# Attention matmuls issued two key chunks behind the scores instead of four, and a reciprocal in two halves, in a pre-norm transformer layer

## What is computed

```python
def attn(x, wq, bq, wk, bk, wv, bv, wo, bo):
    q = einsum('bsd,hde->bhse', x, wq) + bq      # k and v alike
    scores = softmax(einsum('bhse,bhte->bhst', q, k) * 0.125, axis=-1)
    att = einsum('bhst,bhte->bhse', scores, v)
    return att.transpose(0, 2, 1, 3).reshape(b, s, 1024) @ wo.T + bo

def ffn(x):
    h = silu(lin(x, w1)) * lin(x, w2)            # 1024 -> 4096
    h = gelu(lin(h, h1)); h = gelu(lin(h, h2))   # 4096 -> 4096
    return lin(h, w3)                            # 4096 -> 1024

x = x + attn(layernorm(x), ...)
x = x + ffn(layernorm(x))
```

## Time and profile before

| | us |
|---|---|
| median of the two runs shown | 4151.65 (4062.03 and 4241.27) |
| the profiled execution, device time | 3774.29 |
| its span, slowest core (core 7) | 3772.8 |
| spans of the 8 cores | 3759.9 to 3772.8 |
| mean granted TensorE clock of the cores | 0.949 to 0.951 |

### The profile page before, as it was taken

How to read it: one execution, slowest core, us unless ns; L and a number is a source line. 1 busy time by engine, 2 the same in 40 slices (tenths; PEclk the granted TensorE clock), 3 DMA queues, 4 the chain that set the end, 5 groups by cost and what they waited for, 6 DMA issues and landing times.

```text
span 3772.8 us, 35110 instructions; the slowest of 8 cores (3759.9 to 3772.8 us)
## 1 busy us (share of the span) xinstructions
PE 3342.6 (89%) x14676; PEld 1374.5 (36%) x14676; DVE 485.9 (13%) x491; ACT 824.3 (22%) x740; POOL 151.8 (4%) x291
## 2 busy tenths in 40 slices
PE   2377878787768599999999999999999999999999
PEld 0132222222213144444444444444444444444444
DVE  0542222222224413100000000000310000000000
ACT  1106666666761130000000000003000000000000
POOL 0000000000000011000000000001100000000000
PEclk9688989898988699999999999999999999999999
DMA  6000000000102355544444444455554444444445
GB/s 157 0 1 1 1 1 1 1 1 1 23 1 101 97 73 76 93 73 75 78 78 77 73 75 77 85 136 76 75 90 75 78 79 78 72 75 78 78 77 130
DMA packets 49613, 237.41 MB, mean 63 GB/s; under 512 B 7777, under 2 KB 7842, under 8 KB 28338
## 3 DMA queue, kind: packets, MB, share of 16 engines
q0 software_dynamic: 40208, 193.08, 30.1%
q1 hardware_dynamic: 9250, 42.08, 3.3%
HBM read 411.19 MB, written 16.78 MB: 113 GB/s over the span
## 4 chain that ended last, share of the span: by engine, by line
PE 65%; DVE 1%; DMA 1%; ACT 0%; issue 0%; DVEq 0%; ACTq 0%; POOLq 0%
PE ps_f L1167 64%; DMA wb<-h 1%; DVE act_bf L194 1%; PE ps_r L1091 0%; PE ps_m L1087 0%; ACT hbufA L1191 0%; DVE ostg L1218 0%; ACT hbufB L1191 0%; DVEq L193 0%; ACTq L1183 0%; DVEq L1217 0%; DVEq L1215 0%; DVEq L1205 0%; DVEq L1204 0%; POOLq L1132 0%
## 5 line engine op out<-in xcount | busy, mean ns | idle before, releaser
L1167 PE MATMUL ps_f<-hbufB,wb 128*128 128x512 bf16 x5120 | 1109.1, 380 | 11.4 <-DMA wb<-h 8.4
L1167 PE MATMUL ps_f<-hbufA,wb 128*128 128x512 bf16 x4096 | 884.4, 379 | 2.9 <-ACT hbufA L1191 2.9
L1167 PEld LDWEIGHTS ps_f<-hbufB,wb 128*128 128x128 bf16 x5120 | 501.5, 98 | 618.9 <-issue 17.9
L846 ACT ACTIVATE pbuf<-ps_sc,cneg 128x1024 bf16<-128x1024 f32 x512 | 551.8, 1112 | 262.4 <-PE ps_aO L456 250.6
L1167 PEld LDWEIGHTS ps_f<-hbufA,wb 128*128 128x128 bf16 x4096 | 400.6, 98 | 486.7 <-issue 3.9
L1167 PE MATMUL ps_f<-act_bf,wb 128*128 128x512 bf16 x2048 | 451.7, 383 | 19.4 <-DVE act_bf L194 14.3
L456 PE MATMUL ps_aE<-pbuf,vt_sb 128*65 128x512 bf16 x512 | 226.2, 442 | 87.7 <-DVE q_sb L830 87.6
L1167 PEld LDWEIGHTS ps_f<-act_bf,wb 128*128 128x128 bf16 x2048 | 200.8, 98 | 272.3 <-issue 36.2
L435 PE MATMUL ps_sc<-q_sb,k_sb 64*128 64x512 bf16 x1024 | 216.2, 413 | 88.0 <-ACT pbuf L846 78.7
L1218 DVE SCALAR_TENSOR_TENSOR ostg<-ps_f,s_sb,x2rb 128x1024 f32<-128x1024 f32 x16 | 20.6, 1285 | 1987.8 <-PE ps_f L1167 1987.8
L1191 ACT ACTIVATE hbufB<-ps_f,sh_sb 128x1024 bf16<-128x1024 f32 x64 | 71.3, 1114 | 816.0 <-PE ps_f L1167 816.0
(11 more groups left out here) (96 smaller groups left out, 934.4 us busy)
## 6 DMA issues: line engine op xcount, KB each, us to landing
wb<-h POOLq DMA_DIRECT2D x128, 1024.0 KB, 8.0
wb<-w POOLq DMA_DIRECT2D x128, 256.0 KB, 4.2
wb<-w POOLq DMA_DIRECT2D x16, 1024.0 KB, 9.0
xrb<-xst SPq DMA_DIRECT2D x8, 1024.0 KB, 4.8
x2hbm<-x2buf SPq DMA_DIRECT2D x8, 1024.0 KB, 14.5
x2rb<-x2hbm SPq DMA_DIRECT2D x16, 512.0 KB, 9.3
out_fm<-ostg SPq DMA_DIRECT2D x16, 512.0 KB, 8.5
wqld<-wq POOLq DMA_DIRECT2D x1, 2048.0 KB, 16.6
```

What stands on the lines that cost most here:

```text
L846: sc.activation(pbuf[:, (c % 4) * 1024:(c % 4) * 1024 + 1024], ps_sc[:, (c % 2) * 1024:(c % 2) * 1024 + 1024], AF.Exp, bias=cneg[:, j:j + ...
L1167: ins = t.matmul(ps_f[:, (i % 2) * 1024 + nn * 512:(i % 2) * 1024 + (nn + 1) * 512], wb[i % 3][:, k * 128:(k + 1) * 128], rhs[:, k * rstri ...
```

## The change

The order on PE within a unit is rewritten. All 16 scores of a unit are issued in its own loop. With c = 0 and 1 come the attention matmuls of chunks 14 and 15 of the unit before, and from c = 2 those of chunk c-2. The keys of `side` now stand for c itself, so each side item comes two chunks earlier. The last unit issues its last two attention matmuls behind the loop, as before. The waits inside the emit functions are as they were, and so are all buffers. (The branch for items of kind "v" is never taken: no `side` list holds one.)

The reciprocal and its bf16 copy are done for columns 0 to 1023 and then for 1024 to 2047, four vector instructions instead of two, and each ps_rep matmul waits for the half that it reads.

```diff
-                            if I == 0:
-                                emit_scores(t, 0, 0)
-                                emit_scores(t, 0, 1)
-                            for c in range(2, TC):
+                            for c in range(TC):
                                 emit_scores(t, I, c)
-                                if c == 2 and I >= 1:
-                                    emit_att(t, I - 1, TC - 2)
-                                elif c == 3 and I >= 1:
-                                    emit_att(t, I - 1, TC - 1)
-                                if c >= 4:
-                                    emit_att(t, I, c - 4)
-                                for item in side.get(c - 2, ()):
+                                if c <= 1 and I >= 1:
+                                    emit_att(t, I - 1, TC - 2 + c)
+                                if c >= 2:
+                                    emit_att(t, I, c - 2)
+                                for item in side.get(c, ()):
...
-                            if I < NI - 1:
-                                emit_scores(t, I + 1, 0)
-                                emit_att(t, I, TC - 4)
-                                emit_scores(t, I + 1, 1)
-                                emit_att(t, I, TC - 3)
-                            else:
-                                emit_att(t, I, TC - 4)
-                                emit_att(t, I, TC - 3)
+                            if I == NI - 1:
                                 emit_att(t, I, TC - 2, exp_wait=True)
                                 emit_att(t, I, TC - 1, exp_wait=True)
...
+                rhv = [0, 0]
...
-                    vop(v, "reciprocal", denom_sb, denom_sb)
-                    vop(v, "tensor_copy", rtile, denom_sb)
+                    for hf in range(2):
+                        vop(v, "reciprocal", denom_sb[:, hf * 1024:(hf + 1) * 1024],
+                            denom_sb[:, hf * 1024:(hf + 1) * 1024])
+                        rhv[hf] = vop(v, "tensor_copy",
+                                      rtile[:, hf * 1024:(hf + 1) * 1024],
+                                      denom_sb[:, hf * 1024:(hf + 1) * 1024])
...
-                    t.wait_ge(s_v, v0)
                     t.wait_ge(s_small, 16 * 11)
                     for j in range(NPAIR):
...
                         for nn in range(4):
+                            t.wait_ge(s_v, rhv[nn // 2])
                             ins = t.matmul(
```

More of the change, by code:

```diff
@@ L767, in _ @@
                                 side[1] = [("cr", jn)]
-                            if I == 0:
-                                emit_scores(t, 0, 0)
-                                emit_scores(t, 0, 1)
-                            for c in range(2, TC):
+                            for c in range(TC):
                                 emit_scores(t, I, c)
-                                if c == 2 and I >= 1:
-                                    emit_att(t, I - 1, TC - 2)
-                                elif c == 3 and I >= 1:
-                                    emit_att(t, I - 1, TC - 1)
-                                if c >= 4:
-                                    emit_att(t, I, c - 4)
-                                for item in side.get(c - 2, ()):
+                                if c <= 1 and I >= 1:
[3 more added lines that the diff above has]
+                                for item in side.get(c, ()):
                                     kind = item[0]
-                                    if kind == "proj":
+                                    if kind == "v":
+                                        emit_vchunk(t, item[1])
+                                    elif kind == "proj":
                                         emit_proj(t, item[1], item[2], item[3])
```

## The result

The changed kernel is faster: 3684.91 us in the median of 11 runs, against 4097.01 us for 10 runs of the kernel before. In 7 of the 10 runs before and 5 of the 11 after, the cores of one die or of both were granted a lower clock and took longer, whichever the kernel, so I compare the others: 3774 to 3775 us before, 3682 to 3685 us after. Their ratio is 0.9759, with a 95% interval of 0.9743 to 0.9776: 2.4% faster, 91 us of 3775. The profiled execution took 3685.35 us.

What follows compares the result with a forecast made beforehand. In the attention stage a chain of waits between PE and ACT sets the pace. Gains of 63 (steps), 1 (first unit) and 0.7 us (halves), 65 together, take 3774.3 to 3709 us; stated median 4080, range 3700 to 4200 us.

Steps and rivals of the forecast that it cites:

- the bound and the lag: Attention stage: with attention matmuls two chunks behind, ACT becomes the bound; a step falls from 1.15 to 1.007 us.
- the circle: Attention stage: loop of exp, score pair and attention pair, 2.30 us for two exps; without the attention pair 1.74 us.
- the drains' stall: Wait while DVE empties ps_aE and ps_aO between units: 2.64 us beyond a unit's 16 steps, against 2.73 before.
- the projection's own stall: Attention stage, 28 projections: each still holds up ACT about 3.04 us; moving earlier gains only the shorter steps, 0.55 us.
- PE sets that pace in both orders: Attention stage at PE's lower clock: chunks take 1.53 us either way, so 70 gain nothing, taking back 10 us.
- 3 us for the drains behind: Attention stage: 17 drains followed by the lower clock have a longer step after them, taking 3 us off the gain.
- Fewer: Rival, attention stage: no drain ends at the lower clock; gain about 100 us, 3674 us; chance 0.11.
- more drains end at the lower clock: Rival, attention stage: all 31 drains end low, 14 more losing 2.2 us each; gain 34 us, 3740 us; chance 0.18.
- the likeliest case: Whole kernel: the forecast gain of 50 to 85 us, 3689 to 3724 us; chance 0.60.

Runs made afterwards that it cites:

- a4: The kernel before with eight slots for the exponentials instead of four, order on PE unchanged; 3701.2 us.
- a1: The changed kernel with every side item two chunks later, where it was before; 3714.1 us.
- b4: The changed kernel with 10 additional score pairs in every drain of ps_aE and ps_aO, so that PE stays busy; 3647.8 us.
- a3: The kernel before with only the reciprocal and its copy in halves; 3773.8 us.
- b3: The changed kernel with the attention matmuls three chunks behind the scores instead of two; 3710.2 us.

## Why the prediction was right and wrong

**Right: the bound and the lag.** ACT waited for ps_aO because of the slot, the circle opened, PE's pace of 0.87 us fitted under ACT's, and the step fell from 1.15 to 1.00 us. a4 shows the cause by another way to the same step. The lag with the side items at their old place and the halves earns 60 us (a1); the forecast for lag and halves was 64.

**Right: the drains' stall hardly changes.** PE's wait for the casts is 87.2 us after, 87.6 before. The upper-clock step over a drain is 3.51 to 4.17 us in b4, 3.73 in the mean, where I worked out 3.65.

**Right: the halves, as far as can be seen.** Forecast 0.7 us, 0.45 in a3's timeline; in device time so little can't be told from nothing.

**Wrong: "Projections ... the projection's own stall stays about 3.04 us. So all 32 units gain the same."** It holds for 21 of 28. The first projection of each pair now starts with the table load, which the prediction's step never looked at: the load was in no row, and I put it into the forecast of idle time but not into the sum. Seven cases of 1.43 us are 10 us.

**Wrong: "PE sets that pace in both orders ... That takes back 70 x 0.143 = 10 us", and 3 us for the drains behind.** The pace at the lower clock is the same in both, as I said: 1.53 us. But I held the time at the lower clock at its old 166 us, and it fell from 158 to 115. At 0.35 us for each, as b4 gives it, 43 us are 15 us. The rival "Fewer" had the smaller time at the lower clock, with 0.11, and "more drains end at the lower clock" got 0.18, with the idle between S(2) and A(0) growing to 3.0 us as its ground; the clock went the other way. That idle grew only in three drains of the last pair, where no side item is left: 2.99 us after, 2.7 to 2.9 before. In most of the others it is what it was, 2.60, 2.82 or 3.12 us.

Both rivals also counted the wrong thing. I had taken 17 of the 31 drains as ending at the lower clock. The clock records show it within 3 us of 28 of the 31 drains before and of 27 after. So the number of drains hardly changed; what changed is how long the lower clock lasts, 33 stretches of 4.8 us on average before and 28 of 4.1 after.

Which part of the change brought that about is not shown. a1, with the lag alone, stays at 158 us, so the lag with the side items behind the drain does not do it. But a4 gets down to 130 us and moves no side item, so it isn't the move of the projections as such either. The changed kernel and a4 share the faster step and a first projection ahead of the drain; b3 shares both too and has 151 us, with longer steps at the norms' drains. No run separates these.

The two terms bring the sum to 65 + 10 + 15 = 90, and the profiled executions differ by 89. That it fits so closely is partly luck: the lag and the halves earned 60 us (a1) where the forecast had 64, and the side items' place 29 where 1 + 10 + 15 explain 26; and one core's lower clock differs from another's by up to 29 us, which is 9 us of the stage.

**Wrong: the range and the time stated.** I gave 4080 us, the ratio applied to the median of the two runs shown (4062 and 4241), and 3700 us as the lower end, the profiled execution with little more than the forecast gain. The median of 11 runs is 3684.91 us, 15 below that end. An end that rests on the likeliest gain leaves out half of the likeliest case: with "Fewer" it would have been 3674.

**Of the signs in the profile** that I listed: long unbroken rows of exps and ps_sc as the releaser came true; idle time of 180 us was 198; the stage is 87 us shorter, not 64; its clock is 0.92, not 0.90.

**What stays open.** Why the granted clock changes by that much is open. The same pause of 2.60 us ahead of A(0) is followed by the lower clock in one drain and not in another. The earlier trace rows show the first, with matmuls of 0.61 us; the PE row of the drain at the start of the earlier trace rows shows the second, with one of 0.38 us:

```profile
777.37 0.38 PE L456 MATMUL ps_aE<-pbuf,vt_sb 128*65 128x512 bf16 x1 [2.60 <-DVE q_sb L830]
```

The changed kernel has both kinds too, and no run here says which pause does it. Nor is the a1 cost of 29 us split exactly: 43 us of lower clock are 15 us of it by b4's ratio, the table's cover is 10, and that leaves 4.

## What to carry to other kernels

When two engines hand work back and forth, write down the circle with every latency in it, and ask of each member why it is in it; a buffer slot that is freed one step late is as much a member as a data dependency. Where an engine must stand still (a drain, a table load), place its longest independent work there: a projection stalled ACT for 3.0 us in the middle of a unit and for 1.6 us beside a table load, and under a drain the two together stalled it for 2.6 us. And cost a moved side item by what it stands before and behind on every engine, the one that waits for its slot among them.

## What the runs showed that I had not expected

Useless matmuls can pay: 310 score pairs added to the changed kernel (b4) made it 38 us faster. Idle pauses of PE of 2.6 to 3.2 us were mostly followed by the lower clock, at some 0.35 us lost for each us of it.

The activation table was loaded again at the start of each block of ACT's program, 1.28 us each time, although the function stayed the same; one block needed one load.

Exps run closer than one lasts: 1.11 us each in the kernel before and 1.13 on average in the changed one, 1.00 us from start to start. The estimate in the prediction from the Trainium skill ("ScalarE: Activation LUTs", What ACT_TABLE_LOAD costs) was 1.04; its 1.13 for one exp agrees with the second, and for the step the rows decide for the smaller.
